# A state-space kernel: both blocks' convolution on PE, x kept in DRAM between a batch's two FFNs

## The reference

```python
x = x + 0.5 * ffn(layernorm(x))
x = x + attn(layernorm(x))
x = x + 0.5 * ffn(layernorm(x))
# attn: four times
xn = rmsnorm(x, norm_w); xp, z = split(xn @ Win)          # 128 -> 2 * 256
xc = silu(causal_depthwise_conv(xp, conv_w, conv_b))      # 4 taps
dt, Bm, Cm = split(xc @ Wx); delta = softplus(dt @ Wdt + bdt)
y = selective_scan(xc, delta, -exp(A_log), Bm, Cm, Dp)    # h = exp(d*A)*h + d*u*B, y = h.C, 16 states
x = x + (y * silu(z)) @ Wblk
# ffn: for each expert e: silu(x @ Wg[e]) * (x @ Wu[e]) @ Wd[e], weighted by the two top logits' softmax
```

## Time and profile before

| | |
|---|---|
| median of 3 runs | 4576.21 us (4574.02 to 4577.95) |
| the profiled execution | 4581.88 us |
| its span, first to last instruction | 4580.2 us |
| mean granted clock of PE | 0.948 |
| busy: PE, DVE, ACT, POOL | 3945.9, 4067.8, 3346.7, 4095.2 us |

### The profile page before, as it was taken

One profiled execution on the slowest core, in us unless ns is written; L12 is line 12 of the kernel. 1 busy time (PEld: TensorE's weight loads), 2 busy tenths in 40 slices (PEclk: granted clock), 3 DMA queues, 4 the chain that ended last, 5 costly groups with the idle time before them and its releaser, 6 DMA issues.

```text
span 4580.2 us, 48320 instructions
## 1 busy us (share of the span) xinstructions
PE 3945.9 (86%) x11712; PEld 1285.4 (28%) x11712; DVE 4067.8 (89%) x5505; ACT 3346.7 (73%) x5047; POOL 4095.2 (89%) x1804
## 2 busy tenths in 40 slices
PE   7886777898998999899898999899899989678869
PEld 2221222232232323232232323223232322122223
DVE  2668898999999999999999999999999999889963
ACT  4566776777777787777778777787777777667744
POOL 0559999999999999999999999999999999999960
PEclk9897887999999999999999999999999999789969
DMA  2234444354435444544454445444434453443410
GB/s 72 58 74 96 112 100 94 88 114 104 94 90 111 97 94 96 114 95 94 98 111 93 89 105 113 92 91 104 111 87 92 109 113 85 98 100 88 93 46 5
DMA packets 137665, 426.06 MB, mean 93 GB/s; under 512 B 15917, under 2 KB 36334, under 8 KB 137007
## 3 DMA queue, kind: packets, MB, share of 16 engines
q1 hardware_dynamic: 137391, 422.97, 40.8%
HBM read 146.09 MB, written 8.39 MB: 34 GB/s over the span
## 4 chain that ended last, share of the span: by engine, by line
POOL 31%; DVE 25%; issue 17%; PE 16%; ACT 9%; DMA 1%; SPq 1%; DVEq 0%; ACTq 0%; POOLq 0%
POOL work L873 18%; POOL work L864 11%; DVE work L685 10%; DVE dA_ps L685 7%; PE d_ps L400 3%; ACT dA_ps L522 2%; DVE work L690 2%; PE a_ps L393 2%; DVE sg_sb L769 2%; ACT L550 2%; PE a_ps L387 2%; PE b_ps L387 1%; PE y_ps L371 1%; PE b_ps L393 1%; PE s_ps L470 1%
## 5 line engine op out<-in xcount | busy, mean ns | idle before, releaser
L873 POOL TENSOR_TENSOR work<-dd_sb,bc_sb 128x2048 f32<-128x2048 f32 x512 | 2318.8, 4529 | 127.1 <-PE y_ps L371 62.1
L522 ACT ACTIVATE dA_ps<-dd_sb,a_sb 128x512 f32<-128x512 f32 x2048 | 1370.7, 684 | 488.2 <-DVE work L690 298.0
L685 DVE TENSOR_TENSOR_SCAN work<-dA_ps,work 128x512 f32<-128x512 f32 x1408 | 1650.7, 1205 | 62.8 <-POOL work L873 36.6
L864 POOL TENSOR_TENSOR work<-work,bc_sb 128x1024 f32<-128x1024 f32 x704 | 1655.7, 2359 | 13.2 <-DVE work L685 11.9
L685 DVE TENSOR_TENSOR_SCAN dA_ps<-dA_ps,work 128x512 f32<-128x512 f32 x640 | 780.8, 1220 | 12.3 <-ACT dA_ps L522 6.1
L400 PE MATMUL d_ps<-sg_sb,wd_sb 128*128 128x512 f32 (+1 forms) x1536 | 728.7, 605 | 44.2 <-DVE sg_sb L769 44.2
L371 PE MATMUL y_ps<-work,sel_sum 128*32 128x512 f32 x4096 | 594.0, 654 | 88.6 <-POOL work L864 56.5
L387 PE MATMUL b_ps<-xT_sb,wg_sb 128*128 128x512 f32 (+1 forms) x768 | 433.9, 647 | 95.9 <-ACT sg_sb L549 91.8
L387 PE MATMUL a_ps<-xT_sb,wg_sb 128*128 128x512 f32 (+1 forms) x768 | 431.5, 644 | 97.1 <-ACT sg_sb L549 96.2
L690 DVE TENSOR_TENSOR work<-dA_ps,bc_sb 128x512 f32<-128x512 f32 x640 | 438.7, 685 | 11.8
L393 PE MATMUL a_ps<-xs_sb,wu_sb 128*128 128x512 f32 (+1 forms) x768 | 419.7, 629 | 20.4 <-DVE sg_sb L769 15.9
(11 more groups left out here) (116 smaller groups left out, 3820.7 us busy)
## 6 DMA issues: line engine op xcount, KB each, us to landing
dd_sb<-dd_src SPq DMA_DIRECT2D x512, 512.0 KB, 8.6
bc_sb<-bc_rows SPq DMA_DIRECT2D x256, 512.0 KB, 5.7
xr_sb<-in_L_attn_x SPq DMA_DIRECT2D x16, 256.0 KB, 2.8
bc_rows<-dbc_sb SPq DMA_DIRECT2D x128, 32.0 KB, 1.7
out<-xr_sb SPq DMA_DIRECT2D x16, 256.0 KB, 2.2
wg_sb<-in_L_ffn_Wg SPq DMA_DIRECT2D x1, 1376.0 KB
wu_sb<-in_L_ffn_Wu SPq DMA_DIRECT2D x1, 1376.0 KB
wd_sb<-in_L_ffn_Wd SPq DMA_DIRECT2D x2, 512.0 KB
```

What stands on the lines that cost most here:

```text
L522: act.activation(dA_ps[:, g % NDA, :], dd_sb[:, b, c, 0, :], ACT.Exp, scale=a_sb[:, l, b, j, c:c + 1]).then_inc(dA_ready, 1)
L685: dve.tensor_tensor_scan(dA if on_dve(i) else tile, dA, tile, 0.0, ALU.mult, ALU.add).then_inc(scanned, 1)
L864: pool.tensor_tensor(work[:, g % RING], work[:, g % RING], bc_sb[:, j, 0, :].unsqueeze(1).broadcast_to([128, 2, T]), ALU.mult).then_inc(po ...
L873: pool.tensor_tensor(work[:, g % RING:g % RING + 2].rearrange("p h c t -> p (h c) t"), dd_sb[:, b, :, 1, :], bc_sb[:, j, 1, :].unsqueeze(1 ...
```

## The change

PE makes xp1 as it makes xp0, with four shifted products; the folded weights `wconv_sb` and the weights `win0_sb` that they are folded from become twice as wide, and so do the load of `conv_rows` and DVE's fold. `cw_sb`, `xpad`, ACT's copy for block 1 and DVE's three taps are dropped; sq is written to where xn goes later. For the room in SBUF, `xr_sb` has four slots: two for the first FFN of a batch, two for the second. After the first FFN x is stored to a DRAM tensor `x1`, and loaded back before the add after the last layer (L719), which now also waits for that load. All tables of places are new.

```diff
 W, PERIOD = 128, 32
-CORE = {"exp": -10, "scan": -1, "dbu": -1, "dve_prod": 0, "pool_prod": 17, "sum": 30, "y0": 87, "y1": 11}
-PREP = {"dc1": 80, "dc0": 63, "sq": -32, "ms": -13, "rms": -8, "xn": 1, "xp0": 16, "conv0": 10, "xp1": 21, "conv1": 24,
-        "silu_xc": 29, "z0": 33, "zc0": 29, "z1": 45, "zc1": 44, "silu_z": 61, "wx": 36, "dbc": 39, "rows": -14, "dt0": 48,
-        "sp0": 48, "delta0": 55, "du0": 59, "dt1": 76, "sp1": 73, "delta1": 80, "du1": 80, "dd0": 36, "dd1": 96, "bc": 56}
-NEAR = {"dc1": 103, "dc0": 81, "sq": 11, "ms": 21, "rms": 28, "xn": 31, "xp0": 37, "conv0": 44, "xp1": 45, "conv1": 53,
-        "silu_xc": 61, "z0": 65, "zc0": 61, "z1": 69, "zc1": 64, "silu_z": 93, "wx": 72, "dbc": 73, "rows": 36, "dt0": 77,
-        "sp0": 81, "delta0": 85, "du0": 85, "dt1": 90, "sp1": 87, "delta1": 91, "du1": 91, "dd0": 58, "dd1": 109, "bc": 46}
-POST = {"wblk": 84, "h": 91, "attn": 102, "x2": 105}
-POST_NEAR = {"wblk": 14, "h": 14, "attn": 35, "x2": 48}
-FFN_AT = {"gb": 5, "xs": 2, "g0": 7, "g1": 10, "g2": 11, "burst": 7, "u0": 13, "u1": 13, "u2": 17, "hh0": 15, "hh1": 16,
-          "hh2": 22, "down": 27}
-START = {"load": -130, "bn": -61, "nb": -49, "xtok": -51, "xt": -40, "xT": -45, "lg": -35, "lg_sb": -35, "mx": -31,
-         "mi": -28, "gap": -20, "we": -26, "eq": -26, "den": -19, "inv": -25, "comb": -19, "ct": -17, "gates": -21}
-END = {"yt": 17, "xo": 30, "bn": 42, "nb": 69, "xtok": 67, "ht": 80, "h": 79, "store": 119, "acc": 9}
+CORE = {"exp": -10, "scan": -2, "dbu": -6, "dve_prod": 0, "pool_prod": 12, "sum": 29, "y0": 86, "y1": 6}
+PREP = {"dc1": 78, "dc0": 63, "sq": -17, "ms": -8, "rms": -9, "xn": 1, "xp0": 17, "conv0": 17, "xp1": 24, "conv1": 26,
+        "silu_xc": 27, "z0": 33, "zc0": 29, "z1": 42, "zc1": 38, "silu_z": 59, "wx": 36, "dbc": 35, "rows": 5, "dt0": 55,
+        "sp0": 49, "delta0": 55, "du0": 59, "dt1": 73, "sp1": 70, "delta1": 81, "du1": 81, "dd0": 34, "dd1": 109, "bc": 47}
+NEAR = {"dc1": 99, "dc0": 84, "sq": 12, "ms": 25, "rms": 29, "xn": 36, "xp0": 43, "conv0": 40, "xp1": 55, "conv1": 55,
+        "silu_xc": 59, "z0": 65, "zc0": 59, "z1": 69, "zc1": 66, "silu_z": 91, "wx": 84, "dbc": 74, "rows": 12, "dt0": 87,
+        "sp0": 76, "delta0": 82, "du0": 82, "dt1": 91, "sp1": 86, "delta1": 95, "du1": 103, "dd0": 52, "dd1": 97, "bc": 50}
+POST = {"x1": -4, "wblk": 88, "h": 91, "attn": 100, "x2": 104}
+POST_NEAR = {"x1": -71, "wblk": 19, "h": 12, "attn": 27, "x2": 28}
+FFN_AT = {"gb": 4, "xs": 2, "g0": 6, "g1": 8, "g2": 8, "burst": 5, "u0": 11, "u1": 13, "u2": 15, "hh0": 13, "hh1": 15,
+          "hh2": 21, "down": 34}
+START = {"load": -130, "bn": -62, "nb": -54, "xtok": -49, "xt": -36, "xT": -45, "lg": -30, "lg_sb": -36, "mx": -33,
+         "mi": -30, "gap": -24, "we": -28, "eq": -26, "den": -23, "inv": -26, "comb": -22, "ct": -18, "gates": -23}
+END = {"yt": 31, "xo": 32, "bn": 46, "nb": 53, "xtok": 60, "ht": 91, "h": 79, "store": 96, "acc": 17}
...
-XSLOTS, HSLOTS = 6, 4
...
+XSLOTS, HSLOTS = 2, 4
...
+def x_slot(kind, n):
+    return XSLOTS * (kind - 1) + n % XSLOTS
...
-        win_sb = sb("win_sb", [128, NL, 3 * 128])
-        wconv_sb = sb("wconv_sb", [128, NL, KC, 128])
+        win_sb = sb("win_sb", [128, NL, NBLK * 128])
...
-        cw_sb = sb("cw_sb", [128, NL, NBLK, KC])
...
-        win0_sb = work[:, 0, 0, :].rearrange("p (l c) -> p l c", l=NL)
+        win0_sb = work[:, 0, :, :].rearrange("p h (l c) -> p (h l) c", l=NL // 2)
...
-        xpad = sb("xpad", [128, KC - 1 + T])
-        sq_sb = xpad[:, KC - 1:]
+        sq_sb = xn_sb
...
-        xr_sb = sb("xr_sb", [128, XSLOTS, TB, D])
+        xr_sb = sb("xr_sb", [128, 2 * XSLOTS, TB, D])
...
-            for dst, src in ((win_sb[:, :, :], Win[:, :, 128:]), (win0_sb[:, :, :], Win[:, :, 0:128]),
-                             (wconv_sb[:, :, :, :].rearrange("p l k c -> p (l k c)"), conv_rows.broadcast_to([128, NL * KC * 128])), (wx_sb[:, :, :, :], Wx), (wdt_sb[0:DTR, :, :], Wdt),
+            for dst, src in ((win_sb[:, :, :], Win[:, :, NBLK * 128:]), (win0_sb[:, :, :], Win[:, :, 0:NBLK * 128]),
+                             (wconv_sb[:, :, :, :].rearrange("p l k c -> p (l k c)"), conv_rows.broadcast_to([128, NL * KC * NBLK * 128])), (wx_sb[:, :, :, :], Wx), (wdt_sb[0:DTR, :, :], Wdt),
                              (wdt_sb[96:97, :, :], bdt), (wblk_sb[:, :, :, :], Wblk), (wout_sb[:, :], Wout),
-                             (bout_sb[:, :], bout), (normw_sb[:, :], norm_w), (cw_sb[:, :, :, :], conv_w),
-                             (cb_sb[:, :, :], conv_b), (a_sb[:, :, :, :, :], A_log), (dp_sb[:, :, :], Dp)):
+                             (bout_sb[:, :], bout), (normw_sb[:, :], norm_w), (cb_sb[:, :, :], conv_b), (a_sb[:, :, :, :, :], A_log), (dp_sb[:, :, :], Dp)):
                 sp.dma_start(dst, src).then_inc(w_scan, 16)
...
             for t in range(FIRST, LAST):
                 if (f := UNIT_OF.get(t - START["load"])) and FFN[f][1] == 1:
                     n = FFN[f][2]
                     if n >= XSLOTS:
+                        sp.wait_ge(x_spilled[n % XSLOTS], 16 * (n // XSLOTS))
+                        sp.wait_ge(xtok_ready, NORM_OF["ln2", FRONT[n - XSLOTS]] + 1)
+                    sp.dma_start(xr_sb[:, x_slot(1, n)], x_rows[n]).then_inc(x_loaded[n % XSLOTS], 16)
+                if (f := UNIT_OF.get(t - E * PERIOD - END["store"])) is not None:
+                    kind, n = FFN[f][1:]
+                    sp.wait_ge(xo_ready, f + 1)
+                    if kind == 1:
+                        sp.dma_start(x1_rows[n], xr_sb[:, x_slot(1, n)]).then_inc(x_spilled[n % XSLOTS], 16)
+                    else:
+                        sp.dma_start(out_rows[n], xr_sb[:, x_slot(2, n)]).then_inc(stored, 16)
+                if (at := post_at(t, "x1")) and PHASE[at[1]][1] == NL - 1:
+                    n = PHASE[at[1]][0]
+                    if n >= XSLOTS:
                         sp.wait_ge(stored, 16 * (n - XSLOTS + 1))
-                    sp.dma_start(xr_sb[:, n % XSLOTS], x_rows[n]).then_inc(x_loaded[n % 2], 16)
-                if (f := UNIT_OF.get(t - E * PERIOD - END["store"])) is not None and FFN[f][1] == 2:
-                    n = FFN[f][2]
-                    sp.wait_ge(xo_ready, f + 1)
-                    sp.dma_start(out_rows[n], xr_sb[:, n % XSLOTS]).then_inc(stored, 16)
+                    sp.wait_ge(x_spilled[n % XSLOTS], 16 * (n // XSLOTS + 1))
+                    sp.dma_start(xr_sb[:, x_slot(2, n)], x1_rows[n]).then_inc(x_back[n % XSLOTS], 16)
...
                 for b in range(NBLK):
                     if at := prep_at(t, f"xp{b}"):
                         k, w = at
+                        ps = fill("s", conv_done, 2 * k + b + 1)
                         pe.wait_ge(xn_ready, k + 1)
-                        if b == 0:
-                            ps = fill("s", conv_0, k + 1)
-                            for tap in range(KC):
-                                last = pe.matmul(ps[:, :], wconv_sb[:, PHASE[w][1], tap, :], xn_pad[:, tap:tap + T],
-                                                 start=(tap == 0), stop=(tap == KC - 1))
-                            last.then_inc(xp_full, 1)
-                        else:
-                            ps = fill("s", conv_step, 3 * k + 3)
-                            pe.matmul(ps[:, :], win_sb[:, PHASE[w][1], 0:128], xn_sb, start=True, stop=True).then_inc(xp_full, 1)
+                        for tap in range(KC):
+                            last = pe.matmul(ps[:, :], wconv_sb[:, PHASE[w][1], tap, b * 128:(b + 1) * 128],
+                                             xn_pad[:, tap:tap + T], start=(tap == 0), stop=(tap == KC - 1))
+                        last.then_inc(xp_full, 1)
...
                     if ft == 2 and at_xc:
                         k, w = at_xc
                         for b in range(NBLK):
-                            if b == 0:
-                                act.wait_ge(conv_0, k + 1)
-                            else:
-                                act.wait_ge(conv_step, 3 * k + 3)
+                            act.wait_ge(conv_done, 2 * k + b + 1)
                             act.activation(xc_sb[:, w % 2, b, :], xc_sb[:, w % 2, b, :], ACT.Silu).then_inc(xc_ready, 1)
...
                     if k > 0:
-                        act.wait_ge(conv_step, 3 * k)
+                        act.wait_ge(z_full, 2 * k)
                     act.activation(sq_sb, h_sb[:, n % HSLOTS, :], ACT.Square).then_inc(sq_ready, 1)
...
-                if at := prep_at(t, "conv0"):
-                    k, w = at
-                    before = phases_until(w - 2)
-                    act.wait_ge(xp_full, 2 * k + 1)
-                    if before:
-                        act.wait_ge(y_skip, 2 * (before - 1) + 1)
-                    act.activation(xc_sb[:, w % 2, 0, :], s_ps[:, :], ACT.Identity,
-                                   bias=cb_sb[:, PHASE[w][1], 0:1]).then_inc(conv_0, 1)
-                if at := prep_at(t, "conv1"):
-                    k, w = at
```

(34 more changed lines are left out.)

36 lines of the change are left out of this document (19 added, 17 removed).

## The result

| | before | after |
|---|---|---|
| median | 4576.21 us | 4697.66 us (4697.02 to 4701.25) |
| span of the profiled execution | 4580.2 us | 4699.5 us |
| mean granted clock of PE | 0.948 | 0.951 |

The ratio is 1.0268, 95% interval 1.0252 to 1.0285: 121 us slower, where 42 were forecast; it lies above the range as well. The forecast held in sign and in the stretch on PE that the products make longer; it was wrong in how far this delays what comes next, in what comes back for it, and so in size.

The account below looks back on a forecast made before the run. Two nearly equal loops bound the kernel: POOL's own work and a slightly longer PE, DVE, ACT, PE loop. Bulk 28, other phases 5, start 6 and 3 gave +42 us on 4576.2: 4618 us, range 4552 to 4665.

Parts of the forecast that it names:

- What bounds before: Bulk, 47 phases of 65.4 us: POOL's own work beside a slightly longer loop PE, DVE, ACT, PE.
- PE's stretch, 22.2 us: From a phase's last sum to the next one's second: 19.94 us grows to 22.2, stalling the fifth dbu at least 0.6.
- scan 10 "1.7 us later": DVE in the bulk: the product with up-projection u1 waits for PE, so scan 10 behind it starts 1.7 us later.
- 0.36 and 0.47 of relief: Taken off the loop per phase: 0.36 us for DVE's new order, 0.47 us for PE's sums no longer waiting for POOL.
- 0.87 shaded to 0.6: Bulk: net loop growth +0.87 us a phase, taken as +0.6 between bounds -0.2 and +1.7; 47 phases give +28 us.
- Outside the bulk, +5 us for 17 phases: Phases before and after the bulk: four products against ACT's copy and three taps, 0.3 us each, range -20 to +25.
- The start, +9: Before and just after the first dbu: longer loads and fold +5.8 us, the first two preparations +3.
- x through DRAM at nothing; SP's new order covered: Transfers cost nothing, at most 35 us if slots are late; dd1 loads land some 4 us before the fifth dbu.
- The clock: Stretches beside the bulk, granted 0.81 and 0.86: denser PE could lift it, returning 5 to 16 us; chance 0.05.
- (c): Rival: the loop in full, 47 x 1.3 = +61 us, 4651 us, or 4680 without the dd1 cover; chance 0.2.
- (a): Rival: PE's gaps swallow the added products and POOL never waits, 4542 us; chance 0.22 with anything beyond -0.2%.
- What would show it: Bulk signs: PE about 94% busy, u0/u1 waits 2 us or more longer, POOL's sum wait 1.5 us, phase 66.2 us.

Follow-up runs that it names:

- the four kernels that moved waits: Changed kernel with gb[0] first, second sum early, or both: ratios 1.0258, 1.0259, 1.0259; kernel before with its second and sixth sums early: 1.0023.
- the products alone: Kernel before with PE making block 1's plain product four times and DVE's taps kept: 4716.53 us, ratio 1.0300.
- four means: Kernel before with PE making the mean-square product four times instead of once: 4689.14 us, ratio 1.0253.
- the two with downs left out: Kernel before without one down product of experts 0 to 6 each: 4577.98 us; kernel before without one of expert 7's: 4572.22 us.
- two others (downs left out): The changed kernel, 4697.66 us, and the changed kernel without one down product of experts 0 to 6 each, 4703.68 us.

## Why the prediction was wrong, point by point

- **What bounds before.** Right in kind: a loop over PE, DVE and ACT sets the pace, and POOL's work does not. The phase is 65.69 us and not 65.4: the 378 dbu counted in the bulk include those at both of its edges.
- **PE's stretch, 22.2 us.** Measured 21.94. Both corrections, 0.78 us into ACT's wait and 0.4 for the z copy (0.58 where it was 0.24), have their rows. The stall at the fifth dbu, "at least 0.6", is 1.11 in the row shown, and taking it away (second sum early) gained nothing.
- **The step that failed: scan 10 "1.7 us later", less 0.36 and 0.47 of relief, then 0.87 shaded to 0.6.** DVE's product in front of scan 10 did come as forecast (from the last sum 16.11 us before, 17.77 in the rows shown, +1.66), but it no longer releases the scan. Before, it and exp 10 ended together; now exp 10 ends 0.35 us after it, since ACT's burst ahead of exp 10 waits 0.83 us for a gate product behind the four new ones. So scan 10 came 2.17 later. Of the relief the 0.36 for the new order on DVE measured 0.21. The 0.47, PE's waits for POOL, did not come at all: in the window of 801 to 3893 us PE's sums waited 29.8 us for POOL, 22.0 before. It was counted as if a wait off the lap could shorten it; the four kernels that moved waits gained nothing. That is +1.97 at full clock; the clock, which the forecast looked for only outside the bulk, takes 0.25 off. And nothing in the rows supported 0.6 over 0.87; it was drawn toward the lower bound, a case that the argument itself had spoken against. Forecast for the bulk 28 us (41 by its own 0.87); at 1.72 it is 47 x 1.72 = 81.
- **Outside the bulk, +5 us for 17 phases.** Measured +26.1 in phases 52 to 62 alone, and the products alone give 22.5 of it on the kernel before (751.3 against 728.8), 2 us each. The trade "2.68 us of products against 3 us of copy and taps" was wrong. The likely reason is the one that the forecast named and put at 0.3 us, that the products stand ahead of the burst there too and the taps didn't; no row was read for it.
- **The start, +9.** Measured +10.7. By parts: ACT's first work after the loads at 33.45 for 30.66 (+2.8, forecast 3.5), the fold 4.43 us for 2.29 (+2.1, forecast 2.3), PE's gate product at 42.46 for 37.54, the first dbu +7.7 (forecast 7.3), the next window +3.0 (forecast 1.5).

The rows of the kernel after on ACT, DVE and PE for this:

```profile
33.45 0.31 ACT L664 ACTIVATE a_sb<-a_sb 128x128 f32<-128x128 f32 x1 [5.66 <-DMA dp_sb<-in_L_attn_Dp]
...
37.38 4.43 DVE L835 TENSOR_TENSOR wconv_sb<-wconv_sb,work 128x4096 f32<-128x4096 f32 x1 [7.84 <-ACT work L669]
...
42.46 2.07 PE L402 MATMUL b_ps<-xT_sb,wg_sb 128*128 128x512 f32 x2 [9.76 <-DVE xs_sb L751]
```

- **x through DRAM at nothing; SP's new order covered.** Right: alone it cost nothing, and no wait of POOL for `dd_sb` stands in the bulk's list. The store lands later in the changed kernel (7.8 us, against 3.3 in the changed kernel with the old places), and no wait for it shows.
- **The clock.** The two stretches at the sides of the bulk went from 0.81 and 0.86 to 0.83 and 0.87, the bulk from 0.99 to 1.00. The Trainium skill's statement (TensorE: Matmul & The Clock Gate, Part 1: The HAM clock gate) that activity releases the clock agrees with the direction. By these rows it bought nothing there, for both stretches got longer. In the bulk, where the forecast saw 0.99 and left it, the time at 1.2 GHz was worth 0.42 us a phase before and 0.17 after.
- **Rivals.** (c) came nearest, "the loop in full", but at 1.3 us where my own upper bound was 1.7. The range ended at 4665 though 1.7 x 47 with the other terms gives 4576 + 80 + 14 = 4670. The 1.7 was a bound without any relief and the measured 1.72 is 2.17 less relief and clock; that they agree is luck. (a), relief wins, fell: PE's gate wait in the stretch swallowed its 0.78 us as forecast, and the phase grew by the rest.
- **What would show it.** DVE's waits for the up-projections grew (bank b 26.5 to 52.6 us in 2000, 0.9 us a phase more, bank a 41.3), POOL's wait for the sums is 1.1 us a phase where some 1.5 were named, and PE went to 92.3% and not 94, because the phase grew more than forecast.

## What to carry to other kernels

Price an instruction that moves between engines by who waits for it in program order, not by how busy its engine is: here 2.7 us of TensorE cost 1.7 us a phase where ScalarE's copy and a burst stood behind them, and 3.0 us could go for nothing where nobody did. Follow each step to the releaser that comes last after the change, not to the one that came last before it. When an argument gives a loop its number, don't shade it toward a bound that the same argument rejects, and let the range reach the upper bound. The longest wait of a view is rarely the cause: ask of each whether its engine is late or only early. And compare phases of one kind at the same granted clock before a few tenths of a microsecond are put down to a cause.

## What the runs showed of the hardware

Three points are worth their numbers. The profile's chain counts the down product (L415) as 5% of the critical path (it ran without a gap before it and after it), and leaving a third of such a product out, in the stretch or outside it, moved no phase at full clock by more than 0.1 us. These static orders repeat: the stretch was 19.94 us in five kernels (before, x in DRAM, four means, and the two with downs left out). The mean of 40 phases doesn't repeat as well: by the number of phases with a stretch at 1.2 GHz alone it moved 0.3 us between two kernels (x in DRAM) and 0.5 us between two others (downs left out), the second time the way that less work for PE gave more low stretches (20 phases for 5, granted clock 0.942 for 0.951 over the whole span).
